# Layer norms inside the stages that read them, semaphores cleared a stage later, a grouped store and another width-64 attention

## What is computed

```python
x = x + _L0_attn_ref(_layernorm(x), ...)   # 16 heads of 64, causal, softmax over the queries (axis=-2)
x = x + _L0_ffn_ref(_layernorm(x), ...)    # swiglu, hidden 384
x = x + _L1_attn_ref(_layernorm(x), ...)   # 16 heads of 8
x = x + _L1_ffn_ref(_layernorm(x), ...)    # swiglu
x = x + _L2_attn_ref(_layernorm(x), ...)   # x + Fourier attention with a running sum
x = x + _L2_ffn_ref(_layernorm(x), ...)    # router, 4 experts that are attentions, top 2
x = x + _L3_attn_ref(_layernorm(x), ...)   # rotary, 16 heads of 8
x = x + _L3_ffn_ref(_layernorm(x), ...)    # 128 -> 512 -> 512 -> 128 with +-1 weights
```

```python
normed = x * jax.lax.rsqrt(jnp.mean(x * x, axis=-1, keepdims=True) + EPS)
scores = jnp.einsum('bqhd,bkhd->bhqk', q, k)
scores = jnp.where(causal_mask, -jnp.inf, scores)
attn = jax.nn.softmax(scores, axis=-2)
z = jnp.einsum('bhqk,bkhd->bqhd', attn, v)
```

## Time and profile before

| | us |
|---|---|
| median of 3 runs | 2612.87 |
| lowest, highest | 2607.69, 2616.51 |
| profiled execution, own time | 2603.38 |
| its span | 2601.7 |
| mean granted TensorE clock | 0.914 of full speed |
| attention64 | 531.9 |
| swiglu f0, f1 | 68.7, 68.8 |
| attention8 a1, a2, a3 | 249.3, 848.8, 289.9 |
| fourier_attention, sign_mlp | 165.1, 156.5 |
| norm stages n1, n2, n3, n5, n6, n7 | 15.0 to 15.7 each |
| norm stage n4 | 19.3 |
| router, prepare | 20.5, 12.4 |
| behind sign_mlp | 10.4 |

### The profile page before, as it was taken

The page is one execution under the profiler, slowest core; times in us unless marked ns, Lnnn a source line. Parts: engine busy times, 40 slices in busy tenths (PEclk is TensorE's granted clock), DMA queues, the critical chain, the costliest instruction groups (busy, mean ns, idle before and its releaser), DMA issues. The chain is left out here.

```text
span 2601.7 us, 67138 instructions
## 1 busy us (share of the span) xinstructions
PE 2231.7 (86%) x20268; PEld 1324.0 (51%) x20281; DVE 1831.3 (70%) x4158; ACT 1447.0 (56%) x3623; POOL 681.7 (26%) x1223
## 2 busy tenths in 40 slices
PE   4999999978599978665599999999999957899697
PEld 3777777755344545343155555555555533444254
DVE  5666666664388935676389999999999925776553
ACT  2555555542167842322178888888888744777331
POOL 2111111110143200000233444334443216562110
PEclk9999999998689979766599999999999976999799
DMA  4000000000144300000244444444444203331001
GB/s 152 1 0 0 0 0 0 0 1 0 37 130 123 106 1 0 1 0 1 77 133 125 124 128 128 130 129 124 128 128 131 91 14 110 112 107 55 1 1 33
DMA packets 194943, 166.63 MB, mean 64 GB/s; under 512 B 14886, under 2 KB 173704, under 8 KB 194824
## 3 DMA queue, kind: packets, MB, share of 16 engines
q1 hardware_dynamic: 194824, 165.13, 20.8%
HBM read 85.75 MB, written 77.63 MB: 63 GB/s over the span
## 5 line engine op out<-in xcount | busy, mean ns | idle before, releaser
L662 DVE TENSOR_REDUCE a_rowmax<-a_psS 128x2 f32<-128x512 f32 x1536 | 965.4, 683 | 204.0 <-PE a_psS L476 202.2
L612 ACT ACTIVATE a_probs<-a_psT 128x512 f32<-128x512 f32 x1536 | 818.1, 600 | 233.8 <-PE a_psT L483 231.9
L476 PE MATMUL a_psS<-stackk,stackq 49*128 49x256 bf16 x3072 | 502.1, 282 | 60.0 <-DMA stackk<-a_scratch 19.3
L483 PE MATMUL a_psT<-stackq,stackk 51*128 51x256 bf16 x3072 | 478.7, 275 | 3.2 <-ACT a_probs L612 2.9
L521 PE MATMUL a_psO<-a_probs,values 128*32 128x256 f32 x6144 | 413.2, 387 | 2.1 <-ACT a_probs L612 2.1
L476 PEld LDWEIGHTS a_psS<-stackk,stackq 49*128 49x128 bf16 x3072 | 222.8, 96 | 313.2 <-DVE a_rowmax L662 119.3
L928 ACT ACTIVATE a_probs<-a_psS,a_negmax 128x256 f32<-128x256 f32 x256 | 121.2, 473 | 258.4 <-DVE a_negmax L952 258.4
L521 PEld LDWEIGHTS a_psO<-a_probs,values 128*32 128x32 f32 x6144 | 161.1, 109 | 145.5 <-issue 54.6
L483 PEld LDWEIGHTS a_psT<-stackq,stackk 51*128 51x128 bf16 x3072 | 219.1, 95 | 25.3 <-ACT a_probs L612 13.4
L724 POOL COPY a_xcur<-xT 128x256 f32 (+1 forms) x96 | 38.0, 396 | 667.2 <-DVE values L670 421.7
L835 POOL TENSOR_TENSOR a_vr<-a_v,a_rsum 128x256 f32<-128x256 f32 x128 | 78.3, 612 | 373.7 <-DVE a_rsum L962 373.7
(11 more groups left out here) (209 smaller groups left out, 4033.8 us busy)
## 6 DMA issues: line engine op xcount, KB each, us to landing
a_scratch<-a_parts SPq DMA_DIRECT2D x192, 192.0 KB, 2.3
stackq<-a_scratch SPq DMA_DIRECT2D x192, 192.0 KB
stackk<-a_scratch SPq DMA_DIRECT2D x192, 192.0 KB
a_scratch<-a_parts SPq DMA_DIRECT2D x192, 128.0 KB, 2.3
a_scratch<-a_parts SPq DMA_DIRECT2D x192, 64.0 KB, 1.9
stackq<-a_negmaxT SPq DMA_DIRECT2D x192, 8.0 KB
out<-x SPq DMA_DIRECT2D x1, 2048.0 KB, 8.7
stackk<-mask_dram SPq DMA_DIRECT2D x64, 8.0 KB
```

The costliest lines, as they stand in the source:

```text
L476: return pe.matmul(psS[score_bank(s, u)[0]][:, t * SEQ:(t + 1) * SEQ], stackq[r:r + MAX_ROW, b, pr, t * P:(t + 1) * P], stackk[r:r + MAX_R ...
L483: return pe.matmul(psT[shifted_bank(s, u)[0]][:, t * SEQ:(t + 1) * SEQ], stackk[r:r + ZERO_ROW, b, pr, t * P:(t + 1) * P], stackq[r:r + ZE ...
L612: act.activation(probs[:, h, :], psT[shifted_bank(s, u)[0]][:, :], ACT.Exp, scale=w.exp_scale).then_inc(exp_done, 1)
L662: dve.tensor_reduce(rowmax[:, s.parity(1), u, :], psS[score_bank(s, u)[0]][:, :].rearrange("p (t k) -> p t k", t=2), AX_X, ALU.max).then_i ...
```

## The change

Four things are done together.

**Norms as parts.** The seven norm stages n1 to n7 go (n0 stays). A class `Norm` holds their pieces, which swiglu, attention8 (a1, a3), fourier_attention, router and sign_mlp call in their own programs: statistics and root first, then group by group normalise (VectorE), turn (TensorE) and keep (ScalarE) between the stage's own work. In attention8 group 0 stands in the lead step -4, groups 1 to 3 in -3, 4 to 7 in -2. The loops of swiglu, fourier_attention and sign_mlp are written out in full (rounds=0).

```diff
+    def normalise(self, dve, g):
+
+        m, b = self.m, g % 2
+        if g >= 2:
+            dve.wait_ge(self.turned_ready, g - 1)
+            if self.add_to_x:
+                dve.wait_ge(self.x_added, g - 1)
+        for k in range(4):
+            t = 4 * g + k
+            last = dve.tensor_scalar(self.xn[:, b, k, :], m.x4[:, g, k, :], self.small[:, 0, t:t + 1], self.small[:, 4, t:t + 1],
+                                     ALU.subtract, ALU.mult)
+        last.then_inc(self.xn_ready, 1)
+        if self.add_to_x:
+            dve.wait_ge(self.xn_ready, g + 1)
+            dve.tensor_tensor(m.xg[:, g, :], m.xg[:, g, :], self.xn[:, b, :, :].rearrange("p k d -> p (k d)"), ALU.add).then_inc(self.x_added, 1)
+
+    def turn(self, pe, g):
+
+        b = g % 2
+        pe.wait_ge(self.xn_ready, g + 1)
+        if g >= 2:
+            pe.wait_ge(self.xT_written, g - 1)
+        for k in range(4):
+            t = pe.transpose(self.turned[b][:, k * D:(k + 1) * D], self.xn[:, b, k, :], self.m.identity[:, :])
+        t.then_inc(self.turned_ready, 1)
+
+    def keep(self, act, g):
+
+        act.wait_ge(self.turned_ready, g + 1)
+        act.activation(self.m.xT8[:, g, :], self.turned[g % 2][:, :], ACT.Copy).then_inc(self.xT_written, 1)
+
...
             def step(s):
+                if s.at == -1:
+                    norm.turn(pe, 0)
                 for c in range(HCH):
                     if s.has(0):
+                        if c == 0:
+                            norm.wait(pe, s.at)
...
+                    if c == 1 and s.has(0) and s.has(1):
+                        norm.turn(pe, s.at + 1)
...
             def step(s):
+                if s.at == -1:
+                    norm.statistics(dve)
+                    norm.normalise(dve, 0)
+                    norm.normalise(dve, 1)
...
+                if s.has(0) and s.has(2):
+                    norm.normalise(dve, s.at + 2)
...
             def step(s):
+                if s.has(2):
+                    norm.turn(pe, s.at + 2)
...
+                if s.at == -3:
+                    norm.statistics(dve)
+                if s.has(3):
+                    norm.normalise(dve, s.at + 3)
...
             def step(s):
+                if s.has(4) and s.at % 2 == 0:
+                    norm.turn(pe, s.at // 2 + 2)
...
+                if s.has(5) and s.at % 2 == 1:
+                    norm.normalise(dve, (s.at + 5) // 2)
...
+        norm = Norm(m, sem, sb, psT[0:2]) if normed else None
...
+                for g in groups_at.get(s.at, ()):
+                    norm.turn(pe, g)
```

```diff
+
+
+def clear_semaphores(block, handles):
+
+
+    @block.sync
+    def _(sp):
...
-    def clear():
-        with nc.Block() as block:
-            @block.sync
-            def _(sp):
-                for h in held:
-                    sp.sem_clear(h)
...
     def begin():
-        ctx.callback(clear)
-        return ctx.enter_context(nc.Block())
+
+        before, m.before = m.before, (held, sems)
+        if before:
+            ctx.callback(before[1].close)
+        block = ctx.enter_context(nc.Block())
+        if before:
+            clear_semaphores(block, before[0])
+        return block
```

```diff
+        @block.sync
+        def _(sp):
+            for g in range(GROUPS):
+                wait_alone(sp, x_updated, g + 1, sp_passed)
+                sp.dma_start(out4[:, g, :, :], m.x4[:, g, :, :]).then_inc(stored, 16)
+            sp.wait_ge(stored, 16 * GROUPS)
```

```diff
-    plan = Plan(jobs=jobs, weights=L0_PAIRS, unroll=L0_PAIRS, first=L0_PAIRS + 2,
-                           rounds=BATCHES - 2, drain=2)
+    plan = Plan(jobs=jobs, weights=L0_PAIRS, unroll=2 * L0_PAIRS, first=L0_PAIRS + 2,
+                rounds=(BATCHES - 2) // 2, drain=2)
+    HALVES = (slice(0, P // 2), slice(P // 2, P))
...
-        xcur = sb("xcur", [P, SEQ])
...
+        xcur = sb("xcur", [P, 2, SEQ])
...
+        def buffer(s, off):
+
+            return (s.at + off) // L0_PAIRS % 2
...
-                pe.matmul(psQ[:, 0:SEQ], w.wq[:, p * P:(p + 1) * P], xcur[:, :], start=True, stop=True)
-                pe.matmul(psQ[:, SEQ:512], w.wk[:, p * P:(p + 1) * P], xcur[:, :], start=True, stop=True).then_inc(qk_projected, 1)
+                x = xcur[:, buffer(s, 1), :]
+                for j, half in enumerate(HALVES):
+                    pe.matmul(psQ[half, 0:SEQ], w.wq[:, p * P + 64 * j:p * P + 64 * j + 64], x, start=True, stop=True,
+                              tile_position=(0, 64 * j), skip_group_check=True)
+                for j, half in enumerate(HALVES):
+                    mm = pe.matmul(psQ[half, SEQ:512], w.wk[:, p * P + 64 * j:p * P + 64 * j + 64], x, start=True, stop=True,
+                                   tile_position=(0, 64 * j), skip_group_check=True)
+                mm.then_inc(qk_projected, 1)
...
-                    mm = pe.matmul(psV[:, t * P:(t + 1) * P], xcur[:, t * P:(t + 1) * P], w.wv[:, p * P:(p + 1) * P], start=True, stop=True)
+                    for j, half in enumerate(HALVES):
+                        mm = pe.matmul(psV[half, t * P:(t + 1) * P], x[:, t * P + 64 * j:t * P + 64 * j + 64], w.wv[:, p * P:(p + 1) * P],
+                                       start=True, stop=True, tile_position=(0, 64 * j), skip_group_check=True)
...
-                    mm = pe.matmul(psX[:, t * D:(t + 1) * D], zT[:, b, t * P:(t + 1) * P], w.wo[:, p, :],
-                                   start=(p == 0 and t == 0), stop=False, skip_group_check=True)
+                    for j, half in enumerate(HALVES):
+                        mm = pe.matmul(psX[half, t * D:(t + 1) * D], zT[:, b, t * P + 64 * j:t * P + 64 * j + 64], w.wo[:, p, :],
+                                       start=(p == 0 and t == 0), stop=False, tile_position=(0, 64 * j), skip_group_check=True)
...
-                        act.activation(probs[:, a, h, 0:SEQ], psS[a][h][:, 0:SEQ], ACT.Exp, bias=negmax[:, a, 2 * h:2 * h + 1],
+                        act.activation(probs[:, a, h, 0:SEQ], psS[a][h][:, 0:SEQ], ACT.Exp, scale=-1.0, bias=negmax[:, a, 2 * h:2 * h + 1],
                                        accum_out=sums[:, a, 2 * h:2 * h + 1])
...
+            def maximum(s, h):
+
+                a = s.parity(0)
+                if s.known(0, 2):
+                    dve.wait_ge(exp_done, s.n(0, 2, h - 3))
+                wait_alone(dve, scores_ready, s.n(0, 2, h + 1), dve_passed)
+                dve.tensor_tensor_reduce(out=psS[a][h][:, 0:SEQ], in0=psS[a][h][:, 0:SEQ], in1=m.causal[:, :], scale=-1.0, scalar=-NEG,
+                                         op0=ALU.add, op1=ALU.min, accum_out=negmax[:, a, 2 * h:2 * h + 1])
+                dve.tensor_tensor_reduce(out=psS[a][h][:, SEQ:384], in0=psS[a][h][:, SEQ:384], in1=m.causal[:, 0:P], scale=-1.0, scalar=-NEG,
+                                         op0=ALU.add, op1=ALU.min, accum_out=negmax[:, a, 2 * h + 1:2 * h + 2]).then_inc(negmax_ready, 1)
...
+            def step(s):
+                if s.has(0):
+                    maximum(s, 0)
+                    maximum(s, 1)
+                if s.has(1):
+                    take_qk(s)
+                    take_v(s)
+                if s.has(0):
+                    invert(s)
+                if s.has(-2) and s.expert(-2) == L0_PAIRS - 1:
+                    update(s)
```

More of the change, by code:

```diff
@@ L287, in pipeline @@
         step(Step(plan, at, None))
-    with engine.Fori(0, plan.rounds) as turns:
-        for u in range(plan.unroll):
-            step(Step(plan, plan.first + u, turns))
+    if plan.rounds:
+        with engine.Fori(0, plan.rounds) as turns:
+            for u in range(plan.unroll):
+                step(Step(plan, plan.first + u, turns))
     for at in range(plan.first + plan.rounds * plan.unroll, plan.jobs + plan.drain):
@@ L646, in step @@
                     exponential(s, u)
+                if s.at == -4 and normed:
+                    norm.root(act)
+                for g in groups_at.get(s.at, ()):
+                    norm.keep(act, g)
             pipeline(act, plan, step)
@@ L714, in step @@
                         output_stats(s)
+                if s.at == -4 and normed:
+                    norm.statistics(dve)
+                for g in groups_at.get(s.at, ()):
+                    norm.normalise(dve, g)
             pipeline(dve, plan, step)
@@ L1032, in step @@
             def step(s):
+                if s.at == -1:
+                    norm.root(act)
+                    norm.keep(act, 0)
                 if s.has(0):
@@ L1039, in step @@
                         act.activation(silu[:, b, :], gate[b][:, :], ACT.Silu).then_inc(silu_ready, 1)
+                        if c == 1 and s.has(1):
+                            norm.keep(act, s.at + 1)
             pipeline(act, plan, step)
@@ L1277, in step @@
             def step(s):
+                if s.at == -4:
+                    norm.root(act)
+                if s.has(4) and s.at % 2 == 0:
+                    norm.keep(act, s.at // 2 + 2)
                 if s.has(0):
```

(4 more changed lines are left out.)

199 lines of the change are left out of this document (122 added, 77 removed).

## The result

| | before | changed |
|---|---|---|
| median | 2610.8 us (4 runs) | 2506.1 us (4 runs) |
| lowest, highest | 2607.7, 2616.5 | 2500.0, 2510.3 |
| span of the profiled execution | 2601.7 | 2507.8 |

The ratio is 0.9594, with a 95% interval of 0.9574 to 0.9614: 104.7 us less by the medians, 93.9 by the two profiled spans. A later set on another occasion gave 2502.1 us, ratio 0.9590 (0.9572 to 0.9608).

What follows compares the result with a forecast made beforehand. TensorE was taken to bound attention64, while norm stages pass each group from VectorE to TensorE to ScalarE. Terms -47 - 13 - 21 + 3 + 6 - 4 - 13 - 5 = -94 took 2612.9 to 2519 us, range 2478 to 2588.

Steps and rivals of the forecast that it cites:

- attention64, -47: attention64: mask off TensorE, VectorE's loop through maxima, q and k bounds a job at 3.70 us; stage 485 us, -47.
- X: attention64, VectorE: time of the four masked maxima with their four reads, taken as 1.64 us, bounds 1.08 to 2.16.
- Rival A: attention64: TensorE still bounds, X under 1.41 us; -78 there, kernel 2488 us; chance 0.20.
- rival D: Whole kernel: longer written-out loops or merged stages' waits take back the gains; -8 to +8, 2613 us; chance 0.04.
- term for the batch ends: attention64: second token buffer ends TensorE's wait for `vr`; of 0.23 us a job for batches and lead, 0.09 kept.
- Rival C: attention64: product halves run one after the other, 5.31 us a job, +159 there, kernel 2725 us; chance 0.06.
- Rival B: attention64: VectorE's loop takes all of the gain, X at its upper end; +17 there, kernel 2583 us; chance 0.20.
- swiglu: f0 and f1: first product starts 10.1 us earlier, seven turns add 3.9; -6.2 to -6.7 each, -13 together.
- attention8 a1 and a3: Lead 10.1 us shorter each, other turns beside a waiting lead; -21 together, from -10 to -28.
- fourier_attention, +3: Start 13.7 us earlier, but running sum 2.7 us late in six steps, +16; net +3, or -14 if none late.
- sign_mlp, +6: Start -10, but turns wait for late normalise, 2.3 us six times and 1.8 at start, +16; net +6 (-10 to +8).
- Stage changes, -13: Ten remaining stage changes: semaphores cleared beside the next stage, 1.3 us saved at each; -13 (0 to -18).

## Why the prediction was right, and where it was not

**attention64, -47: right sum, wrong terms.** The mechanism of the forecast holds: inside the loop, maxima, q, k and the next scores are the bound. Its size does not. X was put at 1.64 and is 1.23: I put a read of the accumulator at ScalarE's 0.10 and the operation at L976's pace; the operation paces like the plain maximum, 0.35 and 0.25, and its read is free. The handoffs went the other way: k to the scores takes 0.235 in the loop where 0.13 was put, and the first maximum starts 1.11 behind the scores (327.98 to 329.09) where 0.86 + 0.13 was put. Together they make 3.45 and not 3.70. TensorE's own job was sized too long, 3.46 for 3.39, because two changes of shape cost 0.22 and not 0.15; mask and shapes, 0.33 + 0.22, make up the way from 3.93. Rival A, TensorE as the bound, is true of the kernel without a loop alone.

A second failure hid the first. I priced the body of 16 jobs at nothing (only rival D named longer loops, without a price), and it costs 32 us by the run without it: 24 in stops and half-clock jobs and 8 in the jobs between, whose k is handed over more slowly. -82 + 32 = -50. That the two cancel is luck. The term for the batch ends was about right: 0.09 us a job was kept, and without the loop 0.12 remains (449.5 / 128 - 3.39); by the run with one buffer the second is worth 13 to 14 us.

**Rival C fell.** Halves run in pairs: two pairs of 256 elements take 0.48 us (L986) where the whole product's two passes take 0.53 with a change of shape (L985 in the run with whole products, 228.08 to 228.61). TensorE's weight loads for k in the job shown above:

```profile
329.10 0.36 PEld L989 LDWEIGHTS a_psQ<-a_xcur,l_wk 128*64 128x64 f32 x4
```

The rule of the Trainium skill ("TensorE: Matmul & The Clock Gate", Part 3) is that weight loads overlap with products in flight only where the row group differs. The trace does not agree: these loads begin at 329.10 while q's products, which use all 128 rows as well, run from 328.83 to 329.48. The whole products are slower by 0.22 us a job. **Rival B**, X at its upper end, did not come about either: X is 1.23, and without the loop VectorE sits idle 0.69 us a job and TensorE is busy 444.2 of 449.5.

**swiglu**, -13 forecast: -18.6 in the table with the gaps to the next stages; undoing the parts gave back 14.2. **attention8 a1 and a3**, -21: -14.8 and -7.2, the gaps included. Both segments scatter: in the nine profiles that leave them and the clearing as changed, a1 takes 251 to 260 us and a3 294 to 301. Against the means, 255 and 297, they gain 13 and 11, the lead of 10 and the shorter gaps.

**fourier_attention, +3, and sign_mlp, +6**: the stalls came where they were put and with about the size given. In fourier_attention 2.7 us late was forecast for six steps, and 12.6 against 9.8 a step came in five; in sign_mlp 2.3 was forecast, and 2.1 came (2.22 behind `stackk` less the handoff's 0.13). sign_mlp cost 3.9 with the store's saving in it, so about 10, more than the upper end of 8: the wait of 2.6 us also let the clock fall behind some turns (2426.45, where four transposes take 0.91 to the next product and not 0.49), which I had not priced.

**Stage changes, -13**: the gaps are 0.3 where 0.7 to 2.0 were; undoing it makes them 12.5 longer in sum and costs 7 to 11 in the median. **Store, -5**: -6.1. **Router, -4**: not told apart from a2's scatter.

## What to carry to other kernels

Before making a loop's body longer, count its instructions on each engine, and afterwards look at the first record behind each branch: here a body of 339 records on one engine stopped them all at each turn, where 275 did not, and a faster instruction sequence with more instructions was the step. When a job's time equals one bound of the forecast, look whether another is met by the same number: here TensorE's 3.46 was forecast, and the 3.45 was the wait for k. When a stage is folded into its reader, put the new wait where the engine waits anyway and its producer where that engine is idle; two such moves were worth 31 us here without touching any computation. And where a sum comes out as forecast, read its terms again: here two errors of over 30 us cancelled.

## What the runs showed that was not expected

- VectorE's branch back to the start of a loop costs 0.25 to 0.28 us with 137 (the kernel before), 172 and 275 records in the body and 2.7 to 3.1 us with 339. ScalarE with 226 records and TensorE's sequencer with 744 (weight loads counted, matmuls not) resumed within 0.21 us in the same loop.
- The value of a masked maximum is written out at no cost in time: 0.14 us long, but the next operation starts with it (329.44).
- The handoff of k from VectorE to TensorE takes at least 0.235 us inside the loop and as little as 0.10 outside. That is why jobs with the same instructions start 3.45 us apart inside it and 3.39 outside.
